# The gated pass's epilogue: over 31 units instead of 23, in pieces of two blocks, its first norm on ScalarE

## The reference, cut to what matters

```python
messages = node_features @ W_msg + b_msg
q = messages @ W_q
k = messages @ W_k
logits = q @ k.T / scale + gate_bias
probs = jax.nn.sigmoid(logits)
gates_masked = probs * adj_matrix * recency_prior          # both are adj here
aggregated = gates_masked @ messages
updated = jax.nn.relu(jnp.concatenate([node_features, aggregated], axis=1) @ W_upd + b_upd)
mu = jnp.mean(updated, axis=-1, keepdims=True)
var = jnp.var(updated, axis=-1, keepdims=True)
out = (updated - mu) * jax.lax.rsqrt(var + LN_EPS) * ln_gamma + ln_beta
...
x = _layernorm(x + out, axis=-1)
```

## Time and profile before

| what | value |
|---|---|
| runs shown | 1667.01 us median of three (1663.84 to 1667.1) |
| the profiled execution | 1666.21 us, its span 1664.4 us |
| TensorE busy | 1609.0 us (97%) |
| VectorE busy | 1212.8 us (73%) |
| ScalarE busy | 1099.7 us (66%) |
| GpSimd busy | 54.2 us (3%) |
| gated pass | from about 913 to 1292 us of the span |

### The profile page before, as it was taken

How to read it: one execution, slowest core, us unless ns; L and a number is a source line. 1 busy time by engine, 2 the same in 40 slices (tenths; PEclk the granted TensorE clock), 3 DMA queues, 4 the chain that set the end, 5 groups by cost and what they waited for, 6 DMA issues and landing times. The chain is left out here.

```text
span 1664.4 us, 19276 instructions
## 1 busy us (share of the span) xinstructions
PE 1609.0 (97%) x7674; PEld 767.7 (46%) x7674; DVE 1212.8 (73%) x1181; ACT 1099.7 (66%) x784; POOL 54.2 (3%) x49
## 2 busy tenths in 40 slices
PE   7999999999999998999999899999999999999997
PEld 4444444444444444444554444444353444444443
DVE  6866538654766478556899598998989986554886
ACT  5667747764878567755667487796878786454743
POOL 2000000000000000000000000100000100000001
PEclk9999999999999999999999999999999999999999
DMA  9979798979799888996878354554545898764972
GB/s 368 414 301 381 284 419 345 371 284 415 286 388 426 340 317 346 382 340 270 321 283 315 129 202 177 177 207 172 201 166 190 322 371 304 268 250 162 363 276 109
DMA packets 67562, 484.56 MB, mean 291 GB/s; under 512 B 7712, under 2 KB 7872, under 8 KB 9232
## 3 DMA queue, kind: packets, MB, share of 16 engines
q1 hardware_dynamic: 66240, 478.70, 74.6%
q0 software_dynamic: 1088, 4.56, 0.8%
q10 hardware_dynamic: 144, 0.07, 0.0%
HBM read 414.09 MB, written 69.21 MB: 290 GB/s over the span
## 5 line engine op out<-in xcount | busy, mean ns | idle before, releaser
L989 DVE SCALAR_TENSOR_TENSOR a_lo<-a_ring,a_hi 128x2048 f16<-128x2048 f32 x320 | 723.9, 2288 | 301.1 <-ACT a_hi L792 296.9
L792 ACT ACTIVATE a_hi<-a_ring 128x2048 f16<-128x2048 f32 x320 | 604.9, 1905 | 279.4 <-PE spare L594 153.2
L594 PE MATMUL acc<-a_hi,y_hi 128*128 128x512 f16 x1536 | 460.5, 381 | 5.5 <-ACT a_hi L792 3.5
L594 PE MATMUL acc<-a_hi,y_lo 128*128 128x512 f16 x1536 | 460.4, 381 | 0.0
L606 PE MATMUL acc<-a_lo,y_hi 128*128 128x512 f16 x1536 | 406.0, 379 | 7.9 <-DVE a_lo L998 4.9
L606 PEld LDWEIGHTS acc<-a_lo,y_hi 128*128 128x128 f16 x1536 | 149.7, 98 | 192.6 <-DVE a_lo L998 8.1
L594 PEld LDWEIGHTS acc<-a_hi,y_lo 128*128 128x128 f16 x1536 | 150.8, 98 | 182.8 <-issue 2.9
L594 PEld LDWEIGHTS acc<-a_hi,y_hi 128*128 128x128 f16 x1536 | 150.5, 98 | 183.2 <-issue 8.1
L1011 DVE SCALAR_TENSOR_TENSOR gates<-gates,a_ring 128x1024 f32<-128x1024 f32 x128 | 156.1, 1220 | 35.1 <-ACT gates L822 34.8
L805 ACT ACTIVATE a_hi<-gates 128x1024 f16<-128x1024 f32 x128 | 134.8, 1053 | 41.1 <-DVE gates L1011 40.9
L998 DVE TENSOR_TENSOR a_lo<-gates,a_hi 128x1024 f16<-128x1024 f32 x128 | 155.8, 1217 | 0.0
(11 more groups left out here) (119 smaller groups left out, 763.6 us busy)
## 6 DMA issues: line engine op xcount, KB each, us to landing
a_ring<-adj_dram SPq DMA_DIRECT2D x326, 1024.0 KB, 7.4
saved_squares<-squares SPq DMA_DIRECT2D x64, 1024.0 KB, 12.7
a_ring<-saved_squares SPq DMA_DIRECT2D x64, 1024.0 KB, 4.8
x_T<-xt_dram SPq DMA_DIRECT2D x4, 512.0 KB, 8.1
x_rows<-x_dram POOLq DMA_DIRECT2D x1, 2048.0 KB, 12.8
out_dram<-x_rows POOLq DMA_DIRECT2D x3, 512.0 KB, 3.0
out_dram<-x_rows SPq DMA_DIRECT2D x2, 256.0 KB, 2.0
w<-W_dram POOLq DMA_DIRECT2D x2, 64.0 KB, 5.2
```

What stands on the lines that cost most here:

```text
L594: mm = pe.matmul(sums[:, h * BANK:(h + 1) * BANK], blk(y[:, y_pass % 2, :], st.j0 + s), slot(a_hi, st)[:, s, h * BANK:(h + 1) * BANK], sta ...
L792: act.activation(slot(a_hi, st), loaded(st), ACT.Copy, scale=2.0 ** A_EXP).then_inc(s_ahi, 1)
L989: dve.scalar_tensor_tensor(out=slot(a_lo, st).rearrange("p s c -> p (s c)"), in0=loaded(st).rearrange("p s c -> p (s c)"), scalar=2.0 ** A ...
```

## The change

The epilogue of the first three gated chunks holds 31 ticks instead of 23. On VectorE the statistics are made two blocks at a time, before units 9 to 12 and 21 to 24; the aggregation stands before units 12 and 25. The eight `times_gamma` and eight `affine_residual` go. In their place ScalarE applies the first norm (`normalise_first`, two blocks before each of units 15 to 18), and VectorE multiplies with gamma and adds the residual by halves of four blocks (before units 17 to 20). `shift` now runs for both norms, before units 15 and 28. `normalise_again` goes in pairs of blocks before units 28 to 31, `y_high` moves to before unit 1 and `y_low` to before unit 2 of the chunk after that. For the third chunk there is none, and those two fall behind the last gated unit, among the splits of pass 7. GpSimd's roots move with their statistics. The last chunk's table keeps its ticks.

```diff
-LENGTH = {0: 1, 1: 4, 2: 3, 3: 3, 4: 7, 5: 10, 6: 23, 7: 4, 8: 9, LAST_GATED: 14}
+LENGTH = {0: 1, 1: 4, 2: 3, 3: 3, 4: 7, 5: 10, 6: 31, 7: 4, 8: 9, LAST_GATED: 14}
...
+            def normalise_first(blocks):
+                def go(p, k):
+                    act.wait_ge(s_shift, 2 * k + 1)
+                    for b in blocks:
+                        op = act.activation(xn[:, b, :], val[:, b, :], ACT.Identity, bias=stats[:, 2, b:b + 1],
+                                            scale=stats[:, 1, b:b + 1])
+                    if blocks[-1] % HB == HB - 1:
+                        op.then_inc(s_first, 1)
+                return go
...
-                    act.wait_ge(s_shift, k + 1)
+                    act.wait_ge(s_shift, min(2 * k + 2, 2 * NC - 1))
...
-                6: {1: [evacuate], 5: [relu], 20: [normalise_again(range(HB))], 21: [normalise_again(range(HB, CB))],
-                    23: [y_high]},
+                6: {1: [evacuate], 5: [relu], 12: [normalise_first([0, 1])], 13: [normalise_first([2, 3])],
+                    14: [normalise_first([4, 5])], 15: [normalise_first([6, 7])], 25: [normalise_again([0, 1])],
+                    26: [normalise_again([2, 3])], 27: [normalise_again([4, 5])], 28: [normalise_again([6, 7])],
+                    30: [y_high]},
...
+            def gamma_half(h):
+                def go(p, k):
+                    dve.wait_ge(s_first, HALVES * k + h + 1)
+                    dve.tensor_tensor(half(xn, h), half(xn, h), gam[:, :].unsqueeze(1).to_broadcast([P, HB, F]),
+                                      ALU.mult).then_inc(s_scaled, 1)
+                return go
+
+            def residual_half(h):
+                def go(p, k):
+                    dve.wait_ge(s_xb, k + 1)
+                    dve.wait_ge(s_scaled, HALVES * k + h + 1)
+                    op = dve.tensor_tensor(half(val, h), half(xn, h), half(x_chunk(p, k), h), ALU.add)
+                    if h == HALVES - 1:
+                        op.then_inc(s_res, 1)
+                return go
...
-            def shift(p, k):
-
-                dve.wait_ge(s_root, nth("root", p, k, 1))
...
+            def shift(run):
+                def go(p, k):
+                    dve.wait_ge(s_root, nth("root", p, k, run))
...
-                6: {8: [ln_moments(0, s_nl, "nonlin")], 10: [times_gamma], 13: [affine_residual],
-                    16: [ln_moments(1, s_res, "resid")], 19: [shift], 23: [y_low]},
+                6: {6: [some_stats(s_nl, "nonlin", [0, 1])], 7: [some_stats(s_nl, "nonlin", [2, 3])],
+                    8: [some_stats(s_nl, "nonlin", [4, 5])], 9: [some_stats(s_nl, "nonlin", [6, 7]), all_stats(0)],
+                    12: [shift(0)], 14: [gamma_half(0)], 15: [residual_half(0)], 16: [gamma_half(1)],
+                    17: [residual_half(1)], 18: [some_stats(s_res, "resid", [0, 1])],
+                    19: [some_stats(s_res, "resid", [2, 3])], 20: [some_stats(s_res, "resid", [4, 5])],
+                    21: [some_stats(s_res, "resid", [6, 7])], 22: [all_stats(1)], 25: [shift(1)], 31: [y_low]},
...
-            stages = {4: {1: [root(0)]}, 5: {2: [root(0)]}, 6: {8: [root(0)], 16: [root(1)]}, 8: {5: [root(0)], 6: [store]},
+            stages = {4: {1: [root(0)]}, 5: {2: [root(0)]}, 6: {9: [root(0)], 22: [root(1)]}, 8: {5: [root(0)], 6: [store]},
```

More of the change, by code:

```diff
@@ L280, in build @@
         s_exponent, s_root, s_shift = sem("exponent_ready"), sem("ln_root"), sem("ln_shift")
-        s_xb = sem("x_plus_beta")
+        s_xb, s_first = sem("x_plus_beta"), sem("first_norm_applied")
         s_yhi, s_y = sem("y_hi_ready"), sem("y_ready")
@@ L900, in residual, with block_stats, join_stats @@
                 dve.tensor_tensor(val[:, :, :], xn[:, :, :], x_chunk(p, k), ALU.add).then_inc(s_res, 1)
-            def moments_of(blocks, before):
+            def block_stats(blocks):
                 for b in blocks:
                     dve.bn_stats(bn[:, b, :], val[:, b, :]).then_inc(s_bn, 1)
+            def join_stats(blocks, before):
                 dve.wait_ge(s_bn, before + len(blocks))
@@ L912, in moments_of, with some_stats, all_stats, go @@
                                   ALU.add).then_inc(s_var, 1)
+            def moments_of(blocks, before):
+                block_stats(blocks)
+                join_stats(blocks, before)
+            def some_stats(ready, stage, blocks):
+                def go(p, k):
+                    dve.wait_ge(ready, nth(stage, p, k))
+                    block_stats(blocks)
+                return go
+            def all_stats(run):
+                def go(p, k):
+                    join_stats(range(CB), CB * (nth("root", p, k, run) - 1))
+                return go
[4 more added lines that the diff above has]
+                                      ALU.mult).then_inc(s_scaled, 1)
+                return go
+            def residual_half(h):
+                def go(p, k):
+                    dve.wait_ge(s_xb, k + 1)
[3 more added lines that the diff above has]
+                        op.then_inc(s_res, 1)
+                return go
             def ln_moments(run, ready, stage):
@@ L947, in affine_residual @@
                 for b in range(CB):
-                    dve.wait_ge(s_scaled, CB * (nth("resid", p, k) - 1) + b + 1)
+                    dve.wait_ge(s_scaled, HALVES * (NC - 1) + b + 1)
                     op = dve.scalar_tensor_tensor(out=val[:, b, :], in0=xn[:, b, :], scalar=stats[:, 1, b:b + 1],
@@ L951, in affine_residual, with go @@
                 op.then_inc(s_res, 1)
-            def shift(p, k):
-                dve.wait_ge(s_root, nth("root", p, k, 1))
-                dve.scalar_tensor_tensor(out=stats[:, 2, :], in0=moments[:, :, 0], scalar=-1.0, in1=stats[:, 1, :],
-                                         op0=ALU.mult, op1=ALU.mult).then_inc(s_shift, 1)
+            def shift(run):
+                def go(p, k):
+                    dve.wait_ge(s_root, nth("root", p, k, run))
+                    dve.scalar_tensor_tensor(out=stats[:, 2, :], in0=moments[:, :, 0], scalar=-1.0, in1=stats[:, 1, :],
+                                             op0=ALU.mult, op1=ALU.mult).then_inc(s_shift, 1)
+                return go
             def qk_low(run, hi, lo, exp):
@@ L981, in _ @@
                 LAST_GATED: {4: [ln_moments(0, s_nl, "nonlin")], 5: [times_gamma], 6: [affine_residual],
-                    8: [ln_moments(1, s_res, "resid")], 10: [shift], 14: [y_low]},
+                    8: [ln_moments(1, s_res, "resid")], 10: [shift(1)], 14: [y_low]},
             }
```

## The result

The changed kernel takes 1675.88 us (median of six runs, 1673.37 to 1681.78) against 1666.17 for the kernel before (six runs, 1659.89 to 1667.63): a ratio of 1.0068, interval 1.0045 to 1.0091. It is slower, as forecast; its time lies above the forecast 1672.5 and inside the range. The profiled execution took 1676.86 us, its span 1675.1.

What follows compares the result with a forecast made beforehand. In the gated pass VectorE was taken to be as full as TensorE, with 3.9 us lost a chunk. 1666.2 + 3.6 (first two chunks) + 2.4 (third chunk and passage) = 1672.2, stated as 1672.5 us; range 1664 to 1680.

Steps and rivals of the forecast that it cites:

- The measure and its limits: Gated chunks: lag is a product's start later than at full lead; about 4.4 us borne, 2.58 when ScalarE holds the sigmoid.
- ledger of lags: One gated chunk, lag at each product's start: 2.55 us at unit 15, 3.63 at unit 27, 5.40 at unit 28.
- tight limit: Where ScalarE itself holds up the sigmoid: only 2.58 us of lag is borne, so 2.8 is lost at unit 28.
- the boundary: Chunk's end into the next chunk's first units: 2.0 us lost at its sigmoid 32, 0.2 at the one after.
- The first two chunks: Units of two chunks: 5.7 us lost in each instead of 3.9, + 1.8 twice, + 3.6 together.
- Third chunk's epilogue: Last chunk's units to pass 7's first product: - 0.55 us until the last logits, then + 1.3.
- The passage: Into pass 7: `y_high` on ScalarE and `y_low` on VectorE run beside each other, + 1.6 us, between 1.1 and 2.6.
- the third rival, the clock: Stops at unit 28 and the passage: fallen clock costs some 1.7 us each, up to 1679 us; chance 0.1.
- The sum: Whole program: 1666.2 + 3.6 + 2.4 = 1672.2 us, stated as 1672.5.
- The tells: Profile after: ScalarE waits about 2.5 us per `shift`, VectorE idles about 2, TensorE over 2 near unit 28, L506 about 2.
- No change: Gated chunks: first chain hidden, chunk loses 3.5 to 4 us as before, passage adds 0 to 2; 1666 to 1669; chance 0.22.
- The gain: Gated chunks: all waits there go as VectorE loses 1.7 us of work a chunk; 1656 us; chance 0.15.

Runs made afterwards that it cites:

- e1: Changed kernel with both `shift` instructions one unit earlier on VectorE, all else the same: 1664.92 us, ratio 0.9984 to the kernel before.
- e6: Changed kernel with `y_high` and `y_low` before unit 31 in all three chunks: 1675.5 us, ratio 1.0042 to the kernel before.
- e9: Changed kernel with only the third chunk's `y_high` and `y_low` moved to before unit 31: 1672.11 us.
- e4: Changed kernel with `y_low` alone one tick earlier, in all chunks: 1676.03 us, ratio 1.0053 to the kernel before.
- e8: Changed kernel with both `shift` a unit before their norms, every piece one tick earlier, third chunk's y before unit 31: 1655.72 us, ratio 0.9931.
- e7: Kernel before with statistics two blocks at a time and a 26-tick epilogue; first norm, gamma and residual unchanged: 1666.26 us, ratio 0.9996.
- e10: Changed kernel with both `shift` one unit earlier and the third chunk's `y_high` and `y_low` before unit 31: 1659.25 us, ratio 0.9958.
- e11: Changed kernel once more, unaltered, run beside two others on the same chip: 1678.04 us, ratio 1.0077 to the kernel before.
- e3: Changed kernel with only the first `shift` one unit earlier: 1669.12 us, ratio 1.0012 to the kernel before.

## Why the prediction was right

The sign held, and in the chunks the mechanism and the size as well. At the passage one term was mis-sized, since a wait was overlooked, and this term makes up more than half of what was lost. That the time still fell inside the range is partly luck: the room above the forecast was meant for the clock. Step by step:

- **The measure and its limits.** The ledger of lags held up over 20 steps: 2.55 forecast at unit 15 and 2.58 measured, 3.63 and 3.46 at unit 27, 5.40 and 5.23 at unit 28. The tight limit for a stop on ScalarE's side gave a loss of 2.8 at unit 28; 2.73 was measured. Logits 17 to 20 lost 0.47 in sum (0.4 forecast), logits 31 and 32 behind the stop 0.13 each (0.26 for both), the boundary 2.08 (2.0), the unit after 0.3 (0.2).
- **The first two chunks.** + 1.8 each was forecast; 92.88 - 91.16 = 1.72 was measured. That their cause is the distance from `shift` to norm was argued in the prediction, and is shown by e1: one unit of distance gives 4.54 us a chunk back.
- **Third chunk's epilogue (in the last chunk's units), up to the first product of pass 7.** - 0.55 and + 1.3 make + 0.75. Measured: 64.45 - 63.50 = 0.95 up to the last logits, and from those 8.01 instead of 8.23 us to the product at 1294.07: sum 0.73. The split between the two looks wrong, and the clock is why. After the stop of 2.56 us the logits of unit 30 took 2.73 instead of 1.46 us, so the last logits came 4.28 us later instead of 2.72; but the sigmoids went on at ScalarE's pace, and what was lost ahead of the last logits came back behind them:

```profile
1281.78 2.73 PE L629 MATMUL spare<-squares 128*128 128x512 f16 x6 [2.56 <-ACT gates L834]
...
1286.06 1.46 PE L629 MATMUL acc<-squares 128*128 128x512 f16 x6
```

In e6, where the clock did not fall at this place, the stretch up to the last logits took 62.89: - 0.61, the forecast's - 0.55.
- **The passage.** This is the term that was mis-sized: + 1.6 forecast between 1.1 and 2.6, about + 7.2 measured (first product to L506 1303.20 - 1294.07 = 9.13 instead of 4.51, and from L506 on 48.98 instead of 46.37). The prediction set `y_high` on ScalarE and `y_low` on VectorE beside each other, each at the price of its own length. But they are linked twice: `y_low` needs `y_high`, and the take-over of the last gated chunk's sums (L698) waits for `y_low` before it overwrites `z_T`. The wait was in sight, as `y_ready` in the order of ScalarE's list, in the row of L698; it had been free before, as `y_low` stood before unit 26. Moved behind the remainders of two `squares` (4.63 us in one row), it became the last to arrive. e9 shows that the 7.2 come of where this chunk's y stands: with its `y_high` and `y_low` before unit 31 both stretches are back at 4.51 and 46.37, and the time is 5.9 us under the changed kernel's (`y_high` up there delays the first product itself, 9.23 us behind the last logits instead of 8.01). That it is the wait for `y_low` is seen in e4, which moves `y_low` alone by one remainder and takes 2.36 us off. What `y_high` costs at its place on ScalarE was not tried apart.
- **Behind the passage.** In the six executions in which L698 waited for `y_low`, 47.5 to 49.0 us pass from L506 to the wait of 2.00; in all the others 46.36 or 46.37. In the changed kernel the granted clock reads so after TensorE's 5.76 us of idling:

```profile
1302.00:1304.00 2.00, 0.80 (x2) 0.47 (x3) 0.02 (x1) 1.88 (x2) 0.00 (x0) 0.50 0.90 332
1304.00:1306.00 2.00, 2.00 (x11) 1.97 (x10) 1.03 (x1) 2.00 (x2) 0.00 (x0) 0.50 0.98 414
1306.00:1308.00 2.00, 2.00 (x11) 2.00 (x11) 2.00 (x2) 2.00 (x2) 0.00 (x0) 0.50 0.18 74
1308.00:1310.00 2.00, 2.00 (x15) 2.00 (x14) 2.00 (x2) 0.54 (x1) 0.00 (x0) 0.72 0.79 217
```

and the pairs of matmuls with `W_upd` (L498) take 0.64 instead of 0.39 us until it comes back:

```profile
1304.03 0.64 PE L498 MATMUL rows<-wupd,x_T 128*128 128x128 f32 x2
...
1309.15 0.39 PE L498 MATMUL rows<-wupd,x_T 128*128 128x128 f32 x2
```

So the third rival, the clock, did get its price at the passage, where TensorE is the slowest behind the stop. At 1.1 to 2.6 us it is a part of the 7.2, and varies from execution to execution.
- **The sum.** 2 x 1.72 + 0.73 + 7.2 = 11.4, which is what the time shows (11.3, interval 7.5 to 15.2). The forecast terms made 6.0.
- **The tells.** ScalarE's waits (2.36 and 2.43), VectorE's idle time (1.94 and 1.95), TensorE's stops near unit 28 and at unit 1 (2.56 and 1.90) came as told; logits 8 to 30 took 60.17 us, over 58. The wait before L506 did not: 5.76, not about 2.
- **The rivals.** No change fell with the 1.72 a chunk. The gain did not come as the change was placed, but e8 shows that it was there to be had. The clock fell at unit 28 without a price in the chunk, as the prediction expected. In the third chunk's units TensorE idled 2.56 us before logits 30 (1188.89), and the stretches there read

```profile
1188.00:1190.00 2.00, 1.11 (x5) 0.56 (x6) 1.13 (x1) 2.00 (x3) 0.00 (x0) 0.92 0.89 377
1190.00:1192.00 2.00, 2.00 (x7) 0.62 (x5) 1.65 (x3) 2.00 (x4) 0.00 (x0) 0.50 0.00 0
1192.00:1194.00 2.00, 2.00 (x8) 0.83 (x7) 1.95 (x2) 2.00 (x4) 0.00 (x0) 0.73 0.13 16
```

while in the second chunk's units the same stop left the clock at 1.00; the two chunks took 92.89 and 92.88 us.

```profile
1096.00:1098.00 2.00, 1.99 (x10) 0.94 (x11) 2.00 (x2) 2.00 (x4) 0.00 (x0) 1.00 0.50 209
```

The Trainium skill, Perfetto Trace Analysis, Optimizing Scalar/DVE Operations, says that offloading work to Scalar may make sense when DVE is saturated, and that breaking up instructions may let work end sooner where Scalar and Vector aren't saturated but cause bubbles on other engines. The prediction left out that second condition. VectorE, whose statistics were broken up, was busy 58.29 of 61 us, and breaking them up alone left the time as it was (e7, ratio 0.9996). Offloading as placed cost 0.68%. The same offloading came to - 0.16% with one unit of distance alone (e1, not clear of zero), to - 0.42% with the third chunk's y out of the passage as well (e10), and to - 0.69% with every piece one tick earlier besides (e8). So these runs agree on the offloading only once the order is right.

What stays open: whether e6's miss of 1.8 us a chunk is all clock; why e11 stands 2.7 us off its sum, and the part of e3's and e6's that their profiled executions don't account for (the clock at other places of the program is the guess, it wasn't tried); and which of its ticks gives e8 the 0.7 us a chunk (88.35 - 87.64) that it has over e10. The traces put all of it at the boundary, where e10 loses 0.98 and e8 0.27.

## What to carry to other kernels

When a step moves from a full engine to a freer one, price the hand-over before the work: here a 0.15 us instruction, issued just ahead of the other engine's use of it, put 4.36 us between two products instead of a unit's 2.59, and one unit of distance cut the wait to 0.16. When a step is moved later, look for everyone who waits on its semaphore, not only for those that stand behind it in the list: a wait that was free for being long done is the one that nobody sees. And keep a ledger of lag with the limit at each place: in the changed kernel's chunks it told which stops hurt, within 0.2 us, and that a stop costs more behind another one. It can still miss one: in e7 it was 0.7 us off at the boundary.

## What the hardware showed that was not expected

The same stop can change TensorE's clock or leave it. At unit 28 of the changed kernel TensorE idled 2.56 us in the second chunk's units and the clock stayed at 1.00; in the third's it was 0.50 in the stretch 1190 to 1192. In e11, the same kernel once more, it stayed at 1.00 at both places. The price was set by what stood behind: nothing over the chunk at unit 28, where TensorE had slack until its next wait; about 1.1 us at one unit of e6, and 1.1 to 2.6 us at the passage, where it had none. The Trainium skill, TensorE: Matmul & The Clock Gate, What's actually happening, says that an idle array is throttled to 1.2 GHz; the 0.50 of these rows agrees, and the chunk that kept its 1.00 after the same idle time shows that not every such stop is followed by a fall.
